# Second residual summed into rows in PSUM by identity and weight products, and experts chosen in three steps instead of two

## What is computed

```python
h = tok(x)                                  # patches @ W.T + b, class token, + positions
h = h + attn(layernorm(h))                  # linear attention by running sums over an image's tokens:
                                            # ((a_b*c_b) @ U_b.T + alpha*(a_t*z_t*c_t) @ U_t.T)/count + bias, then @ Wo.T
h = h + ffn(layernorm(h))                   # 8 experts, each token to its best two
# ffn: logits = rows @ w_router + b_router; gates = softmax; top 2 per token;
#      an expert takes at most 185 tokens in order; gelu(buf @ w1 + b1) @ w2 + b2,
#      weighted by the gates and added up per token
```

## Time and profile before

| | before |
|---|---|
| median of three runs | 159.75 us (159.46 to 163.18) |
| span of the profiled execution | 157.9 us; its own time is given by this span alone |
| TensorE busy | 148.0 us (94%), 982 products |
| VectorE busy | 105.5 us (67%) |
| ScalarE busy | 82.8 us (52%) |
| GpSimd busy | 50.9 us (32%) |
| first product of the expert stage | 65.95 us |
| mean granted TensorE clock | 0.989 |

### The profile page before, as it was taken

One profiled execution on the slowest core, in us unless ns is written; L12 is line 12 of the kernel. 1 busy time (PEld: TensorE's weight loads), 2 busy tenths in 40 slices (PEclk: granted clock), 3 DMA queues, 4 the chain that ended last, 5 costly groups with the idle time before them and its releaser, 6 DMA issues.

```text
span 157.9 us, 2961 instructions
## 1 busy us (share of the span) xinstructions
PE 148.0 (94%) x982; PEld 138.4 (88%) x982; DVE 105.5 (67%) x330; ACT 82.8 (52%) x210; POOL 50.9 (32%) x55
## 2 busy tenths in 40 slices
PE   7999999999999979999999999999999999999950
PEld 6548999899789768899799899999999999999940
DVE  0074994769887898981396859669486694785710
ACT  3222754644317998857066557474682665737100
POOL 6001200505530000005437167084371661604361
PEclk9999999999999999999999999999999999999995
DMA  5999960079000345301499897888868978600422
GB/s 169 406 420 435 394 230 0 0 243 338 5 0 22 138 163 184 116 0 28 97 349 292 272 269 194 269 192 307 269 130 270 262 250 264 131 7 0 48 25 23
DMA packets 16978, 28.46 MB, mean 180 GB/s; under 512 B 1133, under 2 KB 13591, under 8 KB 16585
## 3 DMA queue, kind: packets, MB, share of 16 engines
q1 hardware_dynamic: 14505, 25.49, 46.6%
q0 software_dynamic: 2464, 2.86, 10.6%
HBM read 24.21 MB, written 4.14 MB: 180 GB/s over the span
## 4 chain that ended last, share of the span: by engine, by line
PE 65%; DMA 11%; DVE 7%; ACT 6%; issue 3%; POOL 3%; SPq 1%; POOLq 1%; DVEq 0%
PE ps L1298 20%; PE ps L1333 10%; PE ps L1132 6%; PE ps L1223 6%; DMA w_even<-w 5%; DMA first_t<-first 4%; PE ps L1335 4%; PE ps L1240 3%; ACT xn L556 2%; PE ps L1165 2%; PE ps L1343 2%; PE ps L1310 2%; DMA rows_in<-xrows,src_row 2%; PE ps L1261 2%; ACT xn L565 2%
## 5 line engine op out<-in xcount | busy, mean ns | idle before, releaser
L497 POOL DMA_INDIRECT out_rows<-out_s,dst_row x16 | 23.8, 1485 | 38.4 <-ACT out_s L682 32.1
L658 ACT ACTIVATE first_t<-ps,b_cur 128x186 f32<-128x186 f32 x64 | 23.0, 413 | 23.5 <-PE ps L1298 22.0
L1333 PE MATMUL ps<-hid_hl,split 128*128 128x372 f32 x96 | 29.1, 369 | 0.0
L1335 PE MATMUL ps<-hid_hl,split 128*128 128x186 f32 x96 | 23.9, 249 | 0.0
L1298 PE MATMUL ps<-first_t,patch_t 128*128 128x186 f32 x128 | 21.7, 322 | 0.1
L977 DVE CAST hid_hl<-first_t 128x372 fp32r<-128x372 f32 x28 | 10.7, 383 | 15.9 <-ACT first_t L658 15.9
L1298 PEld LDWEIGHTS ps<-first_t,patch_t 128*128 128x128 f32 x128 | 20.1, 190 | 0.4 <-issue 0.4
L482 POOL DMA_INDIRECT rows_in<-xrows,src_row x14 | 15.6, 1113 | 11.0 <-DVE src_row L945 7.1
L1298 PE MATMUL ps<-first_t,w_even 128*128 128x186 f32 x112 | 18.9, 321 | 0.0
L522 ACT ACTIVATE split<-patch_t 128x512 fp32r<-128x512 f32 (+2 forms) x28 | 14.4, 577 | 8.1 <-DMA patch_t<-patches 5.7
L1335 PEld LDWEIGHTS ps<-hid_hl,split 128*128 128x128 f32 x96 | 18.3, 191 | 0.0
(11 more groups left out here) (179 smaller groups left out, 263.2 us busy)
## 6 DMA issues: line engine op xcount, KB each, us to landing
w_even<-w SPq DMA_DIRECT2D x8, 1024.0 KB, 5.7
patch_t<-w SPq DMA_DIRECT2D x8, 1024.0 KB, 5.5
att<-attn SPq DMA_DIRECT2D x1, 1280.0 KB, 9.4
patch_t<-patches SPq DMA_DIRECT2D x1, 1188.0 KB, 14.0
patch_t<-patches SPq DMA_DIRECT2D x1, 1080.0 KB, 11.5
first_t<-first SPq DMA_DIRECT2D x1, 978.0 KB, 7.0
out_rows<-h SPq DMA_DIRECT2D x2, 384.0 KB, 2.5
xrows<-xn SPq DMA_DIRECT2D x2, 384.0 KB, 3.5
```

The lines of the kernel that those rows point to most:

```text
L497: pool.indirect_dma_start(out=out[:, :], out_offset=bass.IndirectOffsetOnAxis(ap=dst_row[0:SIZES[s], c:c + 1], axis=0), in_=out_s[q][0:SIZ ...
L658: ins = act.activation(hid[:, f, :], bank(pair)[:, (f % 2) * SL:(f % 2 + 1) * SL], ACT.Gelu, bias=b1_cur[q][:, f:f + 1])
L1333: pe.matmul(dst[:, 0:2 * SL], w2_h[q][:, f, cols], hid_hl[:, f].rearrange("p a s -> p (a s)"), start=f == 0, stop=False)
L1335: ins = pe.matmul(dst[:, 0:SL], w2_l[q][:, f, cols], hid_hl[:, f, 0], start=False, stop=f == KF - 1)
```

## The change

The second residual is no longer made with features on the partitions and then turned. For each tile, TensorE sums rows in PSUM: the two halves of the features of `hb_t` (`h_t` plus the output bias, made by GpSimd) times identity with the router's columns beside it (137 columns each), and then `prod` times `uw`, which now has 265 columns: a half of the features, nine router columns, the other half. Groups of three tiles lie at 265 columns from each other in a slot, so that the second tile crosses a bank and its products are cut there; groups of two lie a bank apart. For this "uw" is computed turned, and a new unit "uw2" turns it back behind the second projection and multiplies it by the router's columns; ScalarE scales it. VectorE's "keep2" copies a group's rows with their logits and means into `h2`; squares are taken from there. The normalised rows of A and B are made by GpSimd, those of C and E by ScalarE, all from `h2`. "y", "add_up", "means2" and the held tile go. There are three choices, of tiles 0 to 2, 3 to 5 and 6 to 9, and the two bridging products stand before the second slots unit. SP stores the output rows in two halves each. The factor product of "a" for group E moves into "zc".

```diff
-BRIDGES = {('slots', 0): 2}
+BRIDGES = {('slots', 1): 2}
...
-CHOICES = [(0, 6), (6, 4)]
+CHOICES = [(0, 3), (3, 3), (6, 4)]
...
+HALF = D // 2
+ROW = D + READ
+STRIDES = {3: ROW, 2: 512}
...
-        h2_t = sb("h2_t", [128, KD, N])
+        hb_t = sb("hb_t", [128, KD, N])
...
-        h2 = sb("h2", [TT, NT, D])
+        h2 = sb("h2", [TT, NT, D + 2 * READ])
...
-        uw = sb("uw", [128, D])
+        uw = sb("uw", [128, ROW])
...
+        wr_c = [cst[:, C_WR0], cst[:, C_WR1]]
+        mixed = [cst[:, C_ID.start:C_WR0.stop], cst[:, C_WR1.start:C_ID.stop]]
+        uw_t = wide(prod[:, 0:KD * 2 * R])
...
-        UNITS = [("proj", A, 0), ("mac", 0, 2), ("uw", 0, 1), ("norm1", A, 0), ("proj", B_, 3), ("norm1", B_, 3),
-                 ("xn_t", A, 1), ("proj", C, 2), ("a", A, 0), ("norm1", C, 1), ("xn_t", B_, 3), ("zc", A, 2),
-                 ("zc", B_, 3), ("xn_t", C, 1), ("a", B_, 2), ("norm1", E, 1), ("zc", C, 3), ("y", A, 0), ("y", B_, 2),
-                 ("xn_t", E, 1), ("norm2", A, 0), ("zc", E, 1), ("a", E, 3), ("norm2", B_, 2), ("a", C, 1), ("y", E, 3),
-                 ("y", C, 1), ("norm2", E, 3), ("norm2", C, 1), ("slots", 0, 0), ("pick", 0, 2), ("slots", 1, 0),
-                 ("pick", 1, 2)]
+        UNITS = [("proj", A, 0), ("mac", 0, 2), ("uw", 0, 1), ("norm1", A, 0), ("proj", B_, 3), ("uw2", 0, 1),
+                 ("norm1", B_, 3), ("xn_t", A, 1), ("proj", C, 2), ("a", A, 0), ("norm1", C, 1), ("xn_t", B_, 3),
+                 ("zc", A, 2), ("zc", B_, 3), ("xn_t", C, 1), ("a", B_, 2), ("norm1", E, 1), ("zc", C, 3),
+                 ("norm2", A, 0), ("xn_t", E, 1), ("a", C, 3), ("zc", E, 1), ("norm2", B_, 2), ("norm2", C, 3),
+                 ("slots", 0, 0), ("norm2", E, 1), ("pick", 0, 2), ("slots", 1, 0), ("pick", 1, 2), ("slots", 2, 0),
+                 ("pick", 2, 2)]
...
         DVE_ORDER = [("proj", A), ("uw", 0), ("proj", B_), ("stats1", B_), ("xn_low", A), ("rstd1", B_), ("proj", C),
                      ("stats1", C), ("xn_low", B_), ("rstd1", C), ("sums", A), ("sums", B_), ("stats1", E), ("prod", A),
-                     ("rstd1", E), ("prod", B_), ("add_up", A), ("sums", C), ("add_up", B_), ("sums", E), ("prod", E),
-                     ("rstd2", A), ("prod", C), ("add_up", E), ("rstd2", B_), ("add_up", C), ("choose", 0), ("rstd2", E),
-                     ("place", 0), ("count", 0), ("rstd2", C), ("choose", 1), ("below", 0), ("place", 1), ("count", 1)]
-        ACT_ORDER = [("mac", 0), ("root1", A), ("norm1", A), ("xn_high", A), ("m_high", 0), ("root1", B_), ("norm1", B_),
-                     ("xn_high", B_), ("root1", C), ("norm1", C), ("xn_copy", C), ("root1", E), ("norm1", E), ("xn_copy", E),
-                     ("means2", A), ("squares2", A), ("root2", A), ("keep2", A), ("means2", B_), ("squares2", B_),
-                     ("root2", B_), ("keep2", B_), ("rows2", A), ("means2", E), ("squares2", E), ("root2", E), ("means2", C),
-                     ("rows2", B_), ("squares2", C), ("root2", C), ("rows2", C), ("keep2", E), ("rows2", E), ("keep2", C)]
+                     ("rstd1", E), ("prod", B_), ("sums", C), ("keep2", A), ("prod", C), ("rstd2", A), ("sums", E),
+                     ("prod", E), ("choose", 0), ("keep2", B_), ("keep2", C), ("place", 0), ("count", 0), ("rstd2", B_),
+                     ("keep2", E), ("choose", 1), ("rstd2", C), ("rstd2", E), ("place", 1), ("choose", 2), ("count", 1),
+                     ("place", 2), ("below", 0), ("count", 2)]
+        ACT_ORDER = [("mac", 0), ("root1", A), ("norm1", A), ("uw2", 0), ("xn_high", A), ("m_high", 0), ("root1", B_),
+                     ("norm1", B_), ("xn_high", B_), ("root1", C), ("norm1", C), ("xn_copy", C), ("root1", E),
+                     ("norm1", E), ("xn_copy", E), ("squares2", A), ("root2", A), ("squares2", B_), ("root2", B_),
+                     ("squares2", C), ("root2", C), ("rows2", C), ("squares2", E), ("root2", E), ("rows2", E),
+                     ("exp", 0)]
         POOL_ORDER = (A, B_, C)
+        POOL_ROWS = (A, B_)
+        STORE_ORDER = [("keep2", A), ("keep2", B_), ("rows2", A), ("keep2", C), ("rows2", B_), ("keep2", E), ("rows2", C),
+                       ("rows2", E)]
         EARLY = [("stats1", A), ("rstd1", A)]
...
-            if step in DVE_READS:
+            if step[0] == "rows2" and step[1] in POOL_ROWS:
+                eng.wait_ge(rows_made, POOL_ROWS.index(step[1]) + 1)
+            elif step in DVE_READS:
...
-            return slot("slots", n)[0:TT, 0:CHOICES[n][1] * NE]
+            at = n % 2 * 512
+            return slot("slots", n)[0:TT, at:at + CHOICES[n][1] * NE]
...
+        def halves(row):
+            return row.rearrange("p (h d) -> p h d", h=2)
+        def both_halves(row):
+            return row[:, 0:2 * (HALF + READ)].rearrange("p (h d) -> p h d", h=2)[:, :, 0:HALF]
+        def normal_rows(eng, g):
+            t0, n = GROUPS[g]
+            for t in range(t0, t0 + n):
+                r = rows_of(t)
+                dst, src = halves(xn[0:r, t]), both_halves(h2[0:r, t])
+                mul, add = rstd[0:r, NT + t:NT + t + 1], nmr[0:r, NT + t:NT + t + 1]
+                if g in POOL_ROWS:
+                    ins = eng.tensor_scalar(dst, src, mul, add, ALU.mult, ALU.add)
+                else:
+                    ins = eng.activation(dst, src, ACT.Identity, bias=add, scale=mul)
+            return ins
...
-            for step in ACT_ORDER:
+            for step in STORE_ORDER:
                 if step[0] == "rows2":
                     done(sp, step)
                     store_rows(xrows, xn, *GROUPS[step[1]], rows_stored[step[1]])
                 elif step[0] == "keep2":
                     done(sp, step)
-                    store_rows(out, h2, *GROUPS[step[1]], out_stored)
+                    for h in range(2):
+                        at = h * (HALF + READ)
+                        store_rows(out[:, h * HALF:(h + 1) * HALF], h2[:, :, at:at + HALF], *GROUPS[step[1]], out_stored)
...
+            def add_bias(n):
+                c0, c1 = group_cols(n)
+                drained(pool, "proj", min(n, C))
+                for k in range(KD):
+                    ins = pool.tensor_scalar(hb_t[:, k, c0:c1], h_t[:, k, c0:c1], bias_o[:, k:k + 1], None, ALU.add)
+                ins.then_inc(biased, 1)
+            pool.wait_ge(dve_step, 2)
+            drained(pool, "uw", 0)
+            add_bias(A)
+            add_bias(B_)
...
+            add_bias(C)
+            add_bias(E)
+            pool.wait_ge(biased, len(GROUPS))
...
+            for n in POOL_ROWS:
+                pool.wait_ge(stats2_ready, nth(DVE_ORDER, ("rstd2",), ("rstd2", n)))
+                normal_rows(pool, n).then_inc(rows_made, 1)
...
+            def sum_squares(g):
+                done(act, ("keep2", g))
+                drained(act, "xn_t", g)
                 t0, n = GROUPS[g]
...
+                for t in range(t0, t0 + n):
                     r = rows_of(t)
-                    ins = act.activation(xn[0:r, t], p[0:r, i * D:(i + 1) * D], ACT.Square, bias=read_s[0:r, t, NE:],
-                                         scale=-1.0, accum_out=squares[0:r, t:t + 1])
+                    ins = act.activation(halves(xn[0:r, t]), both_halves(h2[0:r, t]), ACT.Square,
+                                         bias=h2[0:r, t, HALF + NE:HALF + READ], scale=-1.0,
+                                         accum_out=squares[0:r, t:t + 1])
                 ins.then_inc(squared, 1)
...
-            act.wait_ge(below_ready, 1)
-            act.activation(expd[:, :, :], below[:, :, :], ACT.Exp).then_inc(exp_ready, 1)
+                elif kind == "uw2":
+                    p = filled(act, kind, n)
+                    act.wait_ge(dve_step, 1)
+                    act.activation(uw[:, :], p[:, 0:ROW], ACT.Copy, scale=u_scale[:, 0:1]).then_inc(act_drained, 1)
+                elif kind == "exp":
+                    act.wait_ge(below_ready, 1)
+                    act.activation(expd[:, :, :], below[:, :, :], ACT.Exp).then_inc(exp_ready, 1)
...
+            def set_bias():
+                dve.wait_ge(attn_in, 16)
+                dve.scalar_tensor_tensor(u_cat[:, :, 2 * R], vec_t[:, :, T + 3], alpha_s, vec_t[:, :, T + 2],
+                                         ALU.mult, ALU.add).then_inc(bias_ready, 1)
...
+                if i == len(PIECES) - 1:
+                    set_bias()
...
-            def add_up(n):
-                c0, c1 = group_cols(n)
-                p = filled(dve, "y", n)
-                for k in range(KD):
-                    ins = dve.scalar_tensor_tensor(h2_t[:, k, c0:c1], p[:, k * 512:k * 512 + c1 - c0], bias_o[:, k:k + 1],
-                                                   h_t[:, k, c0:c1], ALU.add, ALU.add)
+            def keep2(n):
+                t0, c = GROUPS[n]
+                p = filled(dve, "norm2", n)
+                for r, a, b in tile_parts(t0, t0 + c):
+                    at = row_start(n, a - t0)
+                    if b - a == 1:
```

(64 more changed lines are left out.)

144 lines of the change are left out of this document (58 added, 86 removed).

## The result

The changed kernel takes 166.78 us (166.00 to 167.44, four runs) beside 160.01 for the kernel before (four runs): ratio 1.0444, 95% interval 1.0402 to 1.0486. Run again later (e12) it took 164.89 (164.52 to 166.40), ratio 1.0381 (1.0303 to 1.0458). The forecast was 165.4, range 160.8 to 169.0. Some executions of these kernels are one to three per cent longer, most of them at a lower mean granted clock; they are left out of all ratios, so a ratio need not be the quotient of two medians.

What follows compares the result with a forecast made beforehand. The bound was a VectorE chain of short steps (the ladder) that starts the solid expert stage. The old median 159.75, plus 4.5 for the ladder and 1.2 for TensorE's clock, gave 165.4 us, range 160.8 to 169.0.

Steps and rivals of the forecast that it cites:

- Early part: TensorE's weights unit and new "uw2" before the third projection: fewer bias products, added transposes, net -0.2 us.
- my upper bound of 1.02: GpSimd's bias sums: one 384-column instruction between 0.46 and 1.02 us, all hidden in existing waits, costing nothing.
- Products and copies: TensorE's row products 3.1 us for three tiles; VectorE's copies out of PSUM 0.97 (A), 1.65 (B and C), 0.77 (E).
- The rival of cheap reads from SBUF: VectorE's copies at twice the rate, ScalarE's SBUF reads 0.3 a tile, clock holds: 162.0 us, chance 0.20.
- The lock: Before the experts, VectorE's and ScalarE's lists wait on each other around C's rows and E's squares; last placing 4.2 later.
- masks of the last four tiles ending near 67.5: Sign of being right: VectorE's last placing, at 63.39 in the old trace, ends near 67.55.
- that of the differences: VectorE's differences to the exponent's argument now follow the last placing, putting off the first expert's input by 0.3 us.
- The clock, 1.2: TensorE's clock halves in a 4.1 us hole before tile 3's picking, slowing it: 1.2 us, ends 0 and 6.5.
- My row for it: Old trace at the kernel's end: granted clock drops to half 2.3 us after the last products.
- the ladder's term: VectorE's chain of steps up to the first expert's input gets 4.2 + 0.3 = 4.5 us later.
- The rival that the clock holds: TensorE's clock stays at full speed through the new hole: 164.2 us, chance 0.22.
- The rival by which ScalarE's fullness held the old ladder: ScalarE, not VectorE's list, limited the steps before the experts; freed, the kernel ends near 156, chance 0.13.

Runs made afterwards that it cites:

- e12: The changed kernel itself, unaltered, run again later: 164.89 us, ratio 1.0381.
- e1: Changed kernel plus sixteen products that feed nothing in TensorE's queue between the second slots and the second picking: 164.01 us, ratio 1.0308.
- e2: Changed kernel with E's squares and root moved ahead of C's normalised rows in ScalarE's list, nothing else: 161.25 us, ratio 1.0108.
- e5: e2 with the copies of the rows of B, C and E out of PSUM on ScalarE instead of VectorE: 160.04 us, ratio 1.0058.
- e7: e2 with two choices (tiles 0 to 5, 6 to 9) in place of three: 165.46 us, ratio 1.0372.
- e9: e5 with tiles 3 to 7 in the second choice, two in the last, and C's deviation, differences and countings reordered: 160.14 us, ratio 1.0049.
- e8: Changed kernel plus four products that feed nothing behind the second slots: 165.34 us (two runs), ratio 1.0384.
- e4: Kernel before, with E's inverse deviation behind the first placing on VectorE and E's rows ahead of C's squares on ScalarE: 163.71 us, no ratio.

## Why the prediction was right, point by point

**Early part, -0.2.** From the end of the first projection to C's sums there are 28.51 us before (12.97 to 41.48) and 28.20 to 28.28 in ten of the twelve executions of the new form (28.39 and 28.51 in the others): -0.3. In the changed kernel's own profile it does not show, because the first projection ended 0.47 later.

**GpSimd.** A bias sum of 384 columns took about 1.25 (two in 2.47), above my upper bound of 1.02 from the earlier trace rows; all eight were over at 27.96 and 36.04, ahead of the steps at 29.63 and 37.52, as the forecast had them. The normalised rows took 0.55 to 0.59 a tile, inside the bounds.

**Products and copies.** The unit of three tiles took 3.14 (42.55 to 45.69; forecast 3.1), the copies 0.99, 1.59 and 0.75 (0.97, 1.65 and 0.77). The rival of cheap reads from SBUF wanted copies at twice the rate and 0.3 a tile for ScalarE's rows; the two rows of C took 1.09 (forecast 1.05). It is out.

**The lock, 4.5 with all that stands in the list.** The mechanism is as forecast: the shift of C, rows of C, squares and root of E, the wait of 2.66 (forecast some 2.5), root as releaser. The sign that was to show it, masks of the last four tiles ending near 67.5, is the sum without the clock's share: they ended at 69.67 here. With the clock held (e1) they ended 26.05 after C's product, against 21.91 before, 4.14 later where the forecast had 4.2. Taken apart, it is 2.74 for the lock (e1 to e2) and 1.58 for the longer list without it (e2 against before), 4.32 together. Of the 1.58, 1.15 goes when ScalarE makes three of the four copies (e5); the other 0.43 is not taken apart. The term that was a little too large is that of the differences, 0.24 of VectorE's list and not 0.3 (e2).

**The clock, 1.2.** It fell in the hole, the picking slowed, and the third slots and the last placing came late, by that path and in that order. The size was 1.94 in one execution and 1.42 in another, within the 0 to 2.3 that I gave for this path. By the prediction's own terms the upper bound is not 2.3 but some 2.0: 1.95 for the slow picking, less 0.35 of slack, and 0.36 for the slots product. Nearly all of that came in the first execution, so that taking half was too little. My row for it, the fall 2.3 us after the last products at the end of the kernel, is not a rule (below).

**The sum.** 4.32 and 1.42 to 1.94, less 0.3 in the early part, is 5.4 to 6.0; the forecast had 5.7. That it fits so closely is in part luck, as the two misses point opposite ways: the ladder's term was 0.2 too large, the clock's 0.2 to 0.7 too small. The medians differ by 6.8 in the first measurement (166.78 and 160.01), 1.1 above the forecast, of which the profiled execution shows 0.5 in the first projection and 0.4 in the expert stage, and by 5.5 in the second (164.89 and 159.44). The rival that the clock holds gave 164.2; e1, in which it is held by force, took 164.01. The rival by which ScalarE's fullness held the old ladder, near 156, is out: e2, with the lock gone and ScalarE freed of the copies, is still 1.1% above the kernel before, and e5, with VectorE unburdened as well, 0.6%.

**Expert stage and stores.** From the first expert product on, 91.73 to 92.39 us in all executions but those of e7 (93.20: TensorE waits 0.81 and 0.45 for two inputs that VectorE copies) and e9 (its late marks); no gather waited for the doubled stores in the changed kernel.

## What to carry to other kernels

When two engines go through lists in a fixed order, write down for each step the step of the other list that it waits for, and look for one that waits across something later in the other's list: here one misplaced entry cost 2.7 us by itself, and moving it, with no instruction changed, took back 4.7. A hole that such a wait tears into TensorE's work can cost more by its clock, here another 1.4 to 1.9 us, and goes away with the wait; filling it with products that feed nothing saves the clock's share alone. After that, ask which engine's list is the ladder, and move what another can do: the copies on an idle ScalarE took 1.15 us from the distance.

## What was not expected of the hardware

The fall of the clock in a hole followed no fixed delay. In the same program, with the same hole of 4.20 us, it came about 1.3 us after the last product in one execution and about 3.7 in another; about 3.6 in e8; and in e4 not at all within 2.94 us. It was back at the upper level 3.9, 2.9, 3.8 and 3.7 us after the picking had begun (the changed kernel, e12, e8, e7). The Trainium skill ("TensorE: Matmul & The Clock Gate", Why this matters for your kernels) has it that an idle stretch between bursts brings the lower level; the runs agree that it may. In e7 it came although no single hole was longer than 2.62, and in e4 it did not come in one of 2.94. What fixes the instant was not settled by these runs, so one trace of such a kernel prices the clock only to half a microsecond.

GpSimd took about 1.25 us to add a per-partition value to 384 columns, where its product of two tensors of that width took 1.02 on half of the partitions, and 1.01 on all of them in the changed kernel.
